# The variance of the feed-forward layer norm as a full product, and its inverse root by ln and exp on ScalarE

## The reference

```
def _layer(x, ...):
    ...                                   # windowed attention, 8 heads of 64
    x = x + o @ wo
    h = shift_token(x)                    # half of the features come from the token before
    mu = h.mean(-1, keepdims=True)
    var = h.var(-1, keepdims=True)
    h = (h - mu) / jnp.sqrt(var + 1e-05) * lg + lb
    h = h @ w1 + b1                       # 128 -> 2 * 341
    a, g = jnp.split(h, 2, axis=-1)
    h = a * jax.nn.gelu(g, approximate=False)
    x = x + h @ w2 + b2
```

## Time and profile before

| | |
|---|---|
| Median of 3 runs | 908.14 us (907.81 to 909.36) |
| The profiled execution's own time | 909.96 us |
| Its span in the trace | 908.2 us |
| PE busy | 800.1 us, 88% |
| DVE busy | 664.4 us, 73% |
| ACT busy | 654.3 us, 72% |
| POOL busy | 523.9 us, 58% |
| Feed-forward stage of layer 0 | about 461 to 534 us |
| Feed-forward stage of layer 1 | about 822 to 908 us |

### The profile page before, as it was taken

How to read it: one execution, slowest core, us unless ns; L and a number is a source line. 1 busy time by engine, 2 the same in 40 slices (tenths; PEclk the granted TensorE clock), 3 DMA queues, 4 the chain that set the end, 5 groups by cost and what they waited for, 6 DMA issues and landing times.

```text
span 908.2 us, 26049 instructions
## 1 busy us (share of the span) xinstructions
PE 800.1 (88%) x9848; PEld 610.5 (67%) x9848; DVE 664.4 (73%) x1347; ACT 654.3 (72%) x2053; POOL 523.9 (58%) x521
## 2 busy tenths in 40 slices
PE   4779999779999999999989887999999999988985
PEld 1458778557777778777756545777877777775652
DVE  1577998677887787877457767778787788745765
ACT  2337777479899899889743337989988998974463
POOL 0363333078888888888511017888888888951100
PEclk8899999889999999999999998999999999999997
DMA  9110001012222222222201121222222222222001
GB/s 308 44 45 3 4 4 41 3 47 55 57 57 63 55 58 55 60 57 63 51 18 24 29 63 37 64 53 58 57 61 56 62 52 58 58 51 100 1 36 58
DMA packets 64704, 48.24 MB, mean 53 GB/s; under 512 B 40410, under 2 KB 50948, under 8 KB 64068
## 3 DMA queue, kind: packets, MB, share of 16 engines
q1 hardware_dynamic: 64580, 46.57, 19.9%
HBM read 10.63 MB, written 2.10 MB: 14 GB/s over the span
## 4 chain that ended last, share of the span: by engine, by line
PE 56%; ACT 17%; DVE 16%; issue 7%; POOL 1%; DMA 1%; SPq 1%; DVEq 0%; ACTq 0%; POOLq 0%
PE ps L415 47%; PE ps L425 9%; ACT prob L880 6%; DVE nmax L1130 3%; ACT sq L822 3%; DVE nt L1158 2%; ACT V L849 2%; ACT oT L831 2%; DVE split L970 2%; ACT kT L856 1%; ACT pT L826 1%; DVE prob L1217 1%; DVE split L968 1%; DMA awo<-in_awo 1%; ACT qT L841 1%
## 5 line engine op out<-in xcount | busy, mean ns | idle before, releaser
L880 ACT ACTIVATE prob<-ps,nmax 128x128 f32<-128x128 f32 x512 | 181.8, 374 | 36.7 <-DVE nmax L1130 36.7
L415 PE MATMUL ps<-wqkv,split 128*128 128x512 f32 x576 | 188.2, 438 | 14.2 <-DVE split L970 10.1
L1348 POOL TENSOR_TENSOR prob<-prob,rinv 128x512 f32<-128x512 f32 x128 | 133.9, 1046 | 88.4 <-DVE rinv L1116 45.8
L415 PEld LDWEIGHTS ps<-wqkv,split 128*128 128x128 f32 x576 | 97.5, 195 | 33.5 <-DVE split L970 10.2
L1130 DVE TENSOR_REDUCE nmax<-ps 128x4 f32<-128x512 f32 x128 | 83.6, 686 | 48.3 <-PE ps L415 48.3
L425 PE MATMUL ps<-ident,prob 128*128 128x128 f32 x640 | 98.3, 276 | 13.9 <-POOL prob L1348 13.1
L880 ACT ACTIVATION_READ_ACCUMULATOR prob<-ps,nmax 128x1 f32 x512 | 109.0, 213 | 0.0
L1359 POOL TENSOR_TENSOR qr<-qr,ss 128x512 f32<-128x512 f32 x64 | 66.9, 1046 | 53.7 <-DVE qr L1142 53.7
L425 PEld LDWEIGHTS ps<-ident,prob 128*128 128x128 f32 x640 | 76.2, 142 | 28.3 <-POOL prob L1348 17.4
L415 PE MATMUL ps<-oT,wo 128*128 128x128 f32 x512 | 73.9, 287 | 22.0 <-ACT oT L831 22.0
L826 ACT ACTIVATE pT<-ps 128x512 f32<-128x512 f32 x128 | 80.0, 625 | 10.7 <-PE ps L425 9.1
(11 more groups left out here) (139 smaller groups left out, 1871.9 us busy)
## 6 DMA issues: line engine op xcount, KB each, us to landing
VB<-V SPq DMA_DIRECT2D x129, 128.0 KB, 2.4
kT<-kT SPq DMA_DIRECT2D x65, 128.0 KB, 2.4
XS<-X SPq DMA_DIRECT2D x32, 128.0 KB, 2.3
XS<-X SPq DMA_DIRECT2D x128, 32.0 KB, 1.9
D<-in_xT SPq DMA_DIRECT2D x8, 256.0 KB, 4.4
XS<-in_xT SPq DMA_DIRECT2D x2, 1024.0 KB, 6.7
out_T<-XS SPq DMA_DIRECT2D x8, 256.0 KB, 2.0
raw<-in_wqkv SPq DMA_DIRECT2D x2, 768.0 KB, 4.4
```

The costliest lines, as they stand in the source:

```text
L415: return nc.tensor.matmul(o, l, r, start=start, stop=stop, skip_group_check=True)
L880: nc.scalar.activation(prob[:, par, grp, s * P:(s + 1) * P], ps[:, 4 + grp, s * P:(s + 1) * P], ACT.Exp, bias=nmax[:, par, grp * 4 + s:grp ...
L1348: g.tensor_tensor(p4, p4, rinv[:, slot, 4 * grp:4 * grp + 4].unsqueeze(2).broadcast_to([P, 4, P]), ALU.mult).then_inc(l_prob, 1)
```

## The change

The variance of a chunk becomes one product `mean_w` by the squares, 512 columns, whose result stands on all partitions. ScalarE takes ln of it and exp of -0.5 times that, both over 128x512, and VectorE multiplies the centred chunk with that buffer (in SBUF; `rstd` now names `qr`). The Newton chain, the diagonals on GpSimd, and the spreading product go. In passes 0 to 4 ln and exp stand on ScalarE between the second and the third Gelu, with a load of the ln and exp table set written ahead of them and, by the compiler, a load of Gelu's set behind them. TensorE's mean of chunk j+3 now waits for the ln of chunk j+2 instead of its scaling.

```diff
@@ tensor
                 def variance(j, bank, slot):
                     pe.wait_ge(ln_squared, nb + j + 1)
-                    for k in range(4):
-                        last = mm(ps[:, bank, k:k + 1], sq[:, slot, k * P:(k + 1) * P], mean_c[:])
-                    last.then_inc(ln_var, 1)
+                    mm(ps[:, bank, :], mean_w[:], sq[:, slot, :]).then_inc(ln_var, 1)
...
                 local(TILES, 0)
                 variance(2, 2, 0)
-                pe.wait_ge(ln_rstd, rstd_before(L, 0) + 1)
-                norm_bcast(0, 0, nb, 0)
                 local(TILES + 1, 1)
-                norm_bcast(1, 1, nb, 1)
...
                     if live(j, 3, CHUNKS):
-                        wait(pe, ln_scaled, fb + j + 2)
+                        pe.wait_ge(ln_log, nb + j + 3)
                         mean(j + 3, 0)
...
                     up(2)
-                    if live(j, 2, CHUNKS):
-                        if live(j, 3, CHUNKS):
-                            pe.wait_ge(ln_rstd, rstd_before(L, j + 3) + 1)
-                        norm_bcast(j + 2, par, nb, 0)
@@ scalar
+                def inverse_deviation(j, bank):
+                    act.wait_ge(ln_var, nb + j + 1)
+                    wait(act, ln_rstd, nb + j - 1)
+                    nc.scalar.activation(lnlog[:, j % 2, :], ps[:, bank, :], ACT.Ln, bias=floor[:, 2:3]).then_inc(ln_log, 1)
+                    act.wait_ge(ln_log, nb + j + 1)
+                    wait(act, ln_scaled, nb + j - 1)
+                    nc.scalar.activation(rstd[:, j % 2, :], lnlog[:, j % 2, :], ACT.Exp, scale=-0.5).then_inc(ln_rstd, 1)
...
                         for c, (u, n) in enumerate(PARTS):
+                            if c == 2 and live(j, 3, CHUNKS):
+                                load_exp_and_ln()
+                                inverse_deviation(j + 3, 0)
                             act.wait_ge(ffn_g, NPART * (fb + j) + c + 1)
...
                 local(TILES + 1, 1)
+                act.wait_ge(l_tr, 2 * (base + TILES))
+                for j in range(3):
+                    inverse_deviation(j, j)
                 for j, t in enumerate((tA, tB)):
                     act.wait_ge(ln_scaled, fb + j + 1)
@@ vector
-            def rstd_links(variances, j, w, before, first, last):
...
-                    if live(j, 3, CHUNKS):
-                        links(j + 3, 1, 6, 0)
                     if live(j, 2, CHUNKS):
-                        dve.wait_ge(ln_bcast, nb + j + 3)
+                        dve.wait_ge(ln_rstd, nb + j + 3)
                         wait(dve, ffn_hi, fb + j + 2)
                         wait(dve, ffn_lo, fb + j + 2)
-                        v.tensor_tensor(tA[:], part(D, j + 2, CHUNK), ps[:, 0, :], ALU.mult).then_inc(ln_scaled, 1)
-                    if live(j, 3, CHUNKS):
-                        links(j + 3, 7, 9, 0)
-                    if live(j, 2, CHUNKS):
+                        v.tensor_tensor(tA[:], part(D, j + 2, CHUNK), rstd[:, par, :], ALU.mult).then_inc(ln_scaled, 1)
                         lows(j + 2, par, tA)
...
-                    if live(j, 3, CHUNKS):
-                        links(j + 3, 10, 12, 0)
...
-                links(2, 1, 6, 2)
+                add_to_x(TILES - 1)
                 scaled(0, tA)
-                links(2, 7, 9, 2)
-                add_to_x(TILES - 1)
-                links(2, 10, NEWTON, 2)
                 scaled(1, tB)
                 lows(0, 0, tA)
                 lows(1, 1, tB)
@@ gpsimd
-            def norm_diag(j, slot, used):
...
-                norm_diag(0, 0, nb - 1)
-                norm_diag(1, 1, nb)
...
-                steps(2, CHUNKS - 1, ffn_norm)
```

More of the change, by code:

```diff
@@ L58 @@
 EXP_AND_LN = 6
-MAGIC = float(0x5F3759DF)
 def live(n, k, count):
@@ L96, in build @@
         mean_w = sb("mean_w", [P, P])
-        mean_c = sb("mean_c", [P, 1])
         lmask = sb("lmask", [P, 2 * CHUNK], BF16)
@@ L121, in build @@
         sq = sb("sq", [P, 2, CHUNK])
-        rstd = sb("rstd", [P, TILES])
-        newt = sb("newt", [P, 2, TILES])
+        lnlog = sb("lnlog", [P, 2, CHUNK])
         tA = sb("tA", [P, CHUNK])
@@ L150, in build @@
         hid = prob[:].rearrange("p a b t -> p (a b) t")
-        diag = qr
+        rstd = qr
         x_in = XS[0]
@@ L199, in build @@
         ln_rstd = sem("ln_rstd")
-        ln_diag = sem("ln_diag")
-        ln_bcast = sem("ln_bcast")
+        ln_log = sem("ln_log")
         ln_scaled = sem("ln_scaled")
@@ L280, in build @@
         N_FFN = 3 + NPART
-        NEWTON = 12
-        def rstd_before(L, j):
-            return NEWTON * (L * (CHUNKS - 1) + max(j - 1, 0))
         def xs_before_local(L):
@@ L426, in turn @@
                                         skip_group_check=True)
-            def norm_bcast(n, par, base, bank):
-                pe.wait_ge(ln_diag, base + n + 1)
-                mm(ps[:, bank, :], ones[:], diag[:, par, :]).then_inc(ln_bcast, 1)
             pe.wait_ge(const_made, 1)
@@ L726, in layer @@
                 pe.wait_ge(x_new, x_before_ffn(L))
-                pe.wait_ge(ln_rstd, rstd_before(L, 2) + 1)
-                pe.wait_ge(ln_scaled, fb + 2)
+                pe.wait_ge(ln_log, nb + 3)
                 pe.wait_ge(bias_made, 1 + L)
@@ L938, in _ @@
             v = nc.vector
-            def rstd_links(variances, j, w, before, first, last):
[L944 to L958, removed]
-                        ins = v.scalar_tensor_tensor(u, u, -0.5, y, ALU.mult, ALU.mult)
-                    else:
-                        to = rstd[:, bass.ds(j * 4, w)] if k == NEWTON else y
-                        ins = v.scalar_tensor_tensor(to, u, 1.5, y, ALU.add, ALU.mult)
-                    ins.then_inc(ln_rstd, 1)
             def split_into(slot, src, width, made, value):
@@ L981, in _ @@
             v.memset(floor[:, 2:3], EPS)
-            v.tensor_scalar(mean_c[:], ones[:, 0:1], 1.0 / DIM, None, ALU.mult)
             v.tensor_scalar(mean_w[:], ones[:], 1.0 / DIM, None, ALU.mult).then_inc(mean_made, 1)
@@ L1196, in layer @@
                 gate = L + 1 == DEPTH
-                def links(j, first, last, bank, chunks=1):
-                    if first == 1:
-                        dve.wait_ge(ln_var, nb + j + chunks)
-                    variances = ps[:, bank, 0:4] if chunks == 1 else ps[:, bank:bank + chunks, 0:4]
-                    rstd_links(variances, j, 4 * chunks, rstd_before(L, j), first, last)
                 def lows(j, slot, t):
@@ L1257, in layer @@
                 ffn_weights(L)
-                links(0, 1, NEWTON, 0, 2)
                 centre(nb, 2, shifted(XS[1], 2, CHUNK), 2)
@@ L1263, in scaled @@
                 def scaled(j, t):
-                    dve.wait_ge(ln_bcast, nb + j + 1)
-                    v.tensor_tensor(t[:], part(D, j, CHUNK), ps[:, j, :], ALU.mult).then_inc(ln_scaled, 1)
-                links(2, 1, 6, 2)
+                    dve.wait_ge(ln_rstd, nb + j + 1)
+                    v.tensor_tensor(t[:], part(D, j, CHUNK), rstd[:, j, :], ALU.mult).then_inc(ln_scaled, 1)
+                add_to_x(TILES - 1)
                 scaled(0, tA)
-                links(2, 7, 9, 2)
-                add_to_x(TILES - 1)
-                links(2, 10, NEWTON, 2)
                 scaled(1, tB)
@@ L1308, in _ @@
             last.then_inc(vones_made, 1)
-            def norm_diag(j, slot, used):
-                wait(pool, ln_bcast, used)
-                g.tensor_tensor(diag[:, slot, :].rearrange("p (k t) -> p k t", k=4),
-                                ident[:].unsqueeze(1).broadcast_to([P, 4, P]),
-                                rstd[:, bass.ds(j * 4, 4)].unsqueeze(2).broadcast_to([P, 4, P]),
-                                ALU.mult).then_inc(ln_diag, 1)
             def a_project(j, par):
@@ L1376, in _ @@
                 local(TILES, 0)
-                pool.wait_ge(l_tr, 2 * (base + TILES))
-                nb = L * CHUNKS
-                pool.wait_ge(ln_rstd, rstd_before(L, 2))
-                norm_diag(0, 0, nb - 1)
-                norm_diag(1, 1, nb)
-                def ffn_norm(j, par):
-                    pool.wait_ge(ln_rstd, rstd_before(L, j + 1))
-                    norm_diag(j, par, nb + j - 1)
-                steps(2, CHUNKS - 1, ffn_norm)
 def shape_constants():
```

## The result

| | before | changed |
|---|---|---|
| median of 6 runs | 907.97 (907.37 to 909.36) | 913.0 (911.22 to 914.44) |
| ratio, 95% interval | | 1.005 [1.0035, 1.0066] |
| profiled execution: own time, span, mean clock | 909.96, 908.2, 0.972 | 912.65, 910.8, 0.965 |

A forecast was written before the change was run, and what follows sets the result against it. TensorE bounds passes 1 to 4 before; after the change a loop over ScalarE and VectorE would. Layer 0 -0.66 and layer 1 +3.62 gave +2.96 us, 911.1 us on the median; 8-in-10 range 905.5 to 914.8.

The forecast's parts named there:

- h: Start of the first hidden part of a pass on VectorE, the event followed through both kernels.
- the old fall: Clock fall in pass 6 of layer 0 before the change, behind a 2.18 us wait; its going credited -1.49 us.
- layer 1, pass 4: Silu's set replaces Gelu's, so another load delays the first Gelu, +1.40 on the loop: pass 11.92 us, +1.24.
- layer 1, pass 5: Without ln the pass would shrink 1.69 to 7.21 us, but TensorE at half clock needs 8.6: -0.3.
- the loop: Passes 1 to 4: a closed queue loop over ScalarE and VectorE takes 9.08 us, above TensorE's 8.57.
- Pitch: Time from h to the next h in passes 1 to 4: 9.08 us against 9.24 before; bounds 8.57 and 9.6.
- the start: From ScalarE's last attention output to h of pass 1: 16.09 us against 14.42, +1.67 a layer.
- Rival 2: Feed-forward passes: TensorE's work decides, pitch 8.57 us; -6.5, 901.6 us; chance 0.11.
- rival 3: Hand-overs between engines dearer than the rows: pitch 9.5, 0.4 more in the start; 915.3 us; chance 0.16.
- rival 4: Each table switch on ScalarE costs a further 1.38 us as drain: 30 on top, 941 us; chance 0.03.
- Rival 1: The loop decides, but TensorE's clock stays up in the new waits: -1.4, 906.7 us; chance 0.18.
- I price each fall with the 1.49 of the row: New TensorE waits, at both layers' start and pass 4 of layer 1, each cost 1.49 us; bounds 0, 1.9.

The follow-up runs named there:

- experiment 8: Unread TensorE products put into its waits to hold the clock: in the changed kernel 908.67 us, in the kernel before (two products) 905.68 us.
- experiment 1: Changed kernel with VectorE's low half issued one pass later, behind the first hidden part: 900.27 us, ratio 0.9903.
- experiment 3: Changed kernel plus an unread 128x1024 copy on ScalarE ahead of ln in ten passes: 922.8 us, ratio 1.0163.
- experiment 6: Changed kernel with Relu in place of Gelu, so the two table loads per pass fall away: 896.32 us, ratio 0.9867.
- experiment 2: Table load written twice, in the changed kernel 912.15 us, with the low half one pass later 899.09 us; the extra load left no trace, so both are repeats.
- experiment 4: Changed kernel with low half one pass later, behind the first hidden part, plus the unread 128x1024 ScalarE copy: 907.95 us, ratio 0.9998.
- experiment 5: Changed kernel with low half behind the third hidden part and three unread products per layer: 893.57 us; with the unread ScalarE copy 894.27 us.

## Why the prediction was right, and where it was short

By the steps of the sum, in the profiled executions (changed less before; h as in the prediction; "filled" is the changed kernel of experiment 8):

| step | forecast | changed | filled |
|---|---|---|---|
| layer 0, oT to h of pass 1 | +1.67 | +2.63 | +1.59 |
| layer 0, passes 1 to 4 | -0.64 +1.49 | +0.59 | -0.63 |
| layer 0, pass 5 | -1.69 | -1.56 | -1.56 |
| layer 0, pass 6 (the old fall) | -1.49 | -1.50 | -1.49 |
| layer 1, oT to h of pass 1 | +1.67 | +1.61 | +1.61 |
| layer 1, passes 1 to 3 | -0.48 +1.49 | +0.80 | -0.32 |
| layer 1, pass 4 | +1.24 | +1.12 | +1.11 |
| layer 1, pass 5 | -0.3 | +0.61 | -1.53 |
| both stages | +2.96 | +4.30 | -1.22 |

(Pass 7 of layer 0, pass 6 of layer 1 and what follows are within 0.1; "changed" in both stages, measured from oT to the last hidden part, is +4.32.)

**Right: the loop.** Pitch 9.11 for 9.08, the start 16.01 in layer 1 for 16.09, pass 4 of layer 1 11.80 for 11.92, the low half in pass 5 5.40 behind h for 5.27, the hole ahead of the value side 0.34 for about 0.5, at the place and with the releaser that were named. Each duration came from a row, and the hand-overs as well; none of these is off by more than 0.16 us. Experiments 1, 3 and 6 show that this is the loop and not something that has its length by chance. Rival 2 (TensorE decides) is what experiment 1 makes of the kernel: its 901.6 was near the 900.3 that the move gives. By the time alone rival 3 (915.3) is hardly further from 913.0 than the forecast (911.1); the pitch decides, 9.11 where rival 3 wants 9.5. The drain of rival 4 has no row.

**Right: without clock there is nothing to pay.** Rival 1 gave -1.4 for the kernel whose clock stays up; filled, the two stages come to -1.22. The medians say +1.2 for it, with an interval of -1.5 to +1.4, so they cannot tell this from zero.

**Short: the clock.** The step that was mis-sized is "I price each fall with the 1.49 of the row": three falls, 4.4 us. Changed less filled is 4.30 + 1.22 = 5.5. The fall in pass 1 was priced too high in both layers (changed less filled is 1.22 and 1.12 over these passes): the 1.49 is what fifteen products lost in pass 6 of before, where they stood in the way of everything; pass 1 lengthens only by what ScalarE on the loop waits for the slow products, 1.07 in layer 0 by the rows above. Pass 5 of layer 1 was priced too low (2.14 instead of 1.4): its fifteen products took 5.95 instead of 3.80, with nothing beside them to hide it. And a fourth was missed: 1.04 at the start of layer 0, where TensorE stood 2.00 us ahead of its first mean and the twelve up-projections took 5.46 instead of 3.06. I had followed TensorE from the up-projections on and not looked at what it did before, between the output projection and the first mean; in the trace of before that wait is 1.06 and costs nothing. No single fall is certain, though: the repeat in experiment 2 has none in pass 1, and its fall at the start of layer 0 cost nothing. PE at the start of layer 1 in the changed kernel's execution:

```profile
820.27 1.10 PE L405 MATMUL ps<-XS,mean_w 128*128 128x512 f32 x2 [2.00 <-DMA XS<-X]
822.09 3.07 PE L405 MATMUL ps<-split,w 128*128 128x512 f32 x12 [0.72 <-issue]
```

The same wait, and no fall: twelve products in 3.07, and a start of 16.01. (In the repeat the same twelve took 4.55, and the start 16.20.)

**Open.** The medians are 5.0 apart, the profiled spans 2.6, the two stages 4.3: what lies outside the stages was 1.7 shorter in this execution. The attention has falls of its own: from 540 to 600 us the granted clock is 0.94 in the trace of before and 0.97 in this one. The other runs can't be split by stage. So of the 2 us by which the forecast was short 1.3 is shown in the stages, and the rest lies within the interval. The filled kernels differ by 3.0 in their medians (from different series) and by 3.7 in their spans (907.5 and 903.8), but only by 0.22 from `oT` to the last hidden part in both layers; 1.7 of it is the tail, 13.25 against 11.59 from the last hidden part on. There six products behind a wait of 2.82 took 4.54 in the changed kernel and 2.85 in the one before. Ten other traces, that of before among them, have this fall too (4.24 to 5.49), so the filling does not bring it. The rest lies ahead of the two `oT`, and its cause stays open.

## What to carry to other kernels

When work moves from an engine that bounds to one that waits, write down the queue of each engine for one period and follow the waits until you are back at the instruction that you began with: that loop, not the busy share, is the new bound. Then look at each link that is only an order in a queue, not a need of the data; moving one such instruction made a loss of 5 us into a gain of 8, and moving it past the next wait as well, with three unread products per layer, made 15 of it. Count the waits of TensorE before the ones that you cause too, and where one can't be avoided, unread products in it may be cheaper than the fall.

## What the runs showed of the hardware

- What a wait costs in clock is not told by its length alone. In the changed kernel the clock fell behind waits of 2.00, 2.48, 2.82 and 3.89 us and neither behind 1.50 nor, in layer 1, behind 2.00. In the repeat of the same instructions (the first of experiment 2) it fell behind that wait of 2.00 in layer 1 as well (twelve products in 4.55 instead of 3.07), but not in pass 1, where TensorE waited 2.81 and its nine products took 2.39. What decides was not found.
- Unread products in a wait are cheap: thirteen of them in the changed kernel gave 4.3 us (3.5 against the repeat), two in the kernel before 1.6.
- A switch of the table set costs 1283 ns, with neighbours 0.01 to 0.02 us away on both sides in 17 of the 20 added switches; in the other three ln waits 0.42 to 0.52 behind the load for TensorE's variance. A second load right behind a first one leaves no record and takes no time.
- A copy of 128x1024 on ScalarE took 1.06 us and held the next operation up by 0.97.
- The same instructions in one order took 10.06, in the next 9.34 and in a third 8.50 us per pass (experiments 3, 4 and 5, with the copy; the unread products of the last lie outside passes 2 to 4, where its pitch is taken).
